# A four-layer decoder on one core: coefficient loads of the weight folding moved, half openings of the streamed attentions reordered, and the last experts' down product split into parts

## The reference

```
x = _layernorm(x + _L0_attn_ref(x, ...))      # minGRU, a gated scan
x = _layernorm(x + _L0_xattn_ref(x, ctx, ...))
x = _layernorm(x + _L0_ffn_ref(x, ...))       # butterfly: W_exp, 10 stages, gelu, 10 stages, W_con
x = _layernorm(x + _L1_attn_ref(x, ...))      # 16 heads of 16, causal
x = _layernorm(x + _L1_xattn_ref(x, ctx, ...))
x = _layernorm(x + _L1_ffn_ref(x, ...))       # 8 experts, top 2, gated, and a shared expert
x = _layernorm(x + _L2_attn_ref(x, ...))      # 16 heads of 16, no mask
x = _layernorm(x + _L2_xattn_ref(x, ctx, ...))
x = _layernorm(x + _L2_ffn_ref(x, ...))       # 8 experts, top 2, all computed
x = _layernorm(x + _L3_attn_ref(x, ...))      # window of 64
x = _layernorm(x + _L3_xattn_ref(x, ctx, ...))
x = _layernorm(x + _L3_ffn_ref(x, ...))       # 16 experts, top 4
```

```
def body(acc, expert):
    w1e, b1e, w2e, b2e, ce = expert
    hmid = jax.nn.gelu(x @ w1e + b1e, approximate=False)
    return (acc + (hmid @ w2e + b2e) * ce[:, None], None)
```

## Time and profile before

| what | us |
|---|---|
| median of three runs | 2581.3 |
| the three runs | 2581.3, 2587.81, 2570.56 |
| the profiled execution's own time | 2578.14 |
| its span | 2576.4 |
| PE busy in the span | 2279.8 |
| DVE busy in the span | 1404.3 |
| ACT busy in the span | 1129.9 |

### The profile page before, as it was taken

One profiled execution on the slowest core, in us unless ns is written; L12 is line 12 of the kernel. 1 busy time (PEld: TensorE's weight loads), 2 busy tenths in 40 slices (PEclk: granted clock), 3 DMA queues, 4 the chain that ended last, 5 costly groups with the idle time before them and its releaser, 6 DMA issues. The chain is left out here.

```text
span 2576.4 us, 41981 instructions
## 1 busy us (share of the span) xinstructions
PE 2279.8 (88%) x15258; PEld 1519.6 (59%) x15258; DVE 1404.3 (55%) x3517; ACT 1129.9 (44%) x1927; POOL 644.5 (25%) x868
## 2 busy tenths in 40 slices
PE   1789999998899999949999998799998898699996
PEld 1678754444345799924444444467665545589995
DVE  5625377885464221268999955666566555411114
ACT  6543345655342111135777774522443334234444
POOL 6010232321211033231111002100356311245551
PEclk8789978988998999967999999789999898799998
DMA  6100132220113199832131101031111210599996
GB/s 231 34 1 1 34 55 44 46 46 18 30 35 119 58 332 332 304 105 47 26 51 26 26 7 46 2 115 38 31 27 19 57 18 26 209 297 350 356 342 234
DMA packets 86512, 268.89 MB, mean 104 GB/s; under 512 B 25354, under 2 KB 43906, under 8 KB 70300
## 3 DMA queue, kind: packets, MB, share of 16 engines
q1 hardware_dynamic: 70628, 233.10, 29.6%
q0 software_dynamic: 15680, 33.12, 4.1%
HBM read 207.36 MB, written 23.94 MB: 90 GB/s over the span
## 5 line engine op out<-in xcount | busy, mean ns | idle before, releaser
L1667 ACT ACTIVATE prob<-st_ps 128x1024 f32<-128x1024 f32 x448 | 412.8, 933 | 215.3 <-PE st_ps L1534 213.9
L1687 DVE TENSOR_REDUCE cmax<-ring 128x1 f32<-128x512 f32 x640 | 401.4, 683 | 40.2 <-PE ring L1542 37.7
L3133 PE MATMUL A<-xbT,w 128*128 128x128 f32 x2512 | 301.8, 276 | 1.1 <-DMA w<-L1f_W_dram 0.5
L3133 PEld LDWEIGHTS A<-xbT,w 128*128 128x128 f32 x2512 | 291.6, 193 | 1.9 <-DMA w<-L1f_W_dram 0.8
L1581 PE MATMUL acc<-prob,v 128*32 128x256 f32 (+2 forms) x3200 | 265.5, 405 | 13.6 <-DVE byq L1725 12.6
L3377 DVE COPY yb<-C 128x256 f32<-128x256 f32 x118 | 50.1, 424 | 285.3 <-PE C L3141 282.4
L3050 POOL DMA_INDIRECT y_rows_dram<-yb,dst x118 | 116.3, 986 | 326.1 <-DVE yb L3377 322.9
L3141 PE MATMUL C<-w,hid 128*128 128x256 f32 x632 | 149.3, 379 | 0.0
L1534 PE MATMUL st_ps<-qst,kst 64*128 64x512 f32 (+3 forms) x560 | 135.6, 482 | 7.3 <-DMA qst<-parts 3.2
L3037 POOL DMA_INDIRECT xb<-x_rows_dram,src x118 | 115.0, 975 | 99.7 <-DVE src L3347 64.4
L1683 DVE CUSTOM_DVE_ANT_0 masked<-ring,causal_wide 128x512 bf16<-128x512 f32 (+3 forms) x256 | 112.5, 487 | 44.2 <-PE ring L1542 43.3
(11 more groups left out here) (478 smaller groups left out, 4471.0 us busy)
## 6 DMA issues: line engine op xcount, KB each, us to landing
w<-L3f_W_dram SPq DMA_DIRECT2D x79, 1026.0 KB
w<-L1f_W_dram SPq DMA_DIRECT2D x39, 1536.0 KB
room<-y_rows_dram SPq DMA_DIRECT2D x8, 1024.0 KB, 10.1
kst<-parts SPq DMA_DIRECT2D x120, 64.0 KB, 2.4
qst<-parts SPq DMA_DIRECT2D x120, 64.0 KB, 2.4
gate<-L2f_gates_dram SPq DMA_DIRECT2D x5, 1536.0 KB, 7.4
first<-parts SPq DMA_DIRECT2D x96, 64.0 KB, 2.4
qT<-dense SPq DMA_DIRECT2D x84, 64.0 KB, 2.4
```

The lines of the kernel that those rows point to most:

```text
L1667: act.activation(prob[:, step % PROBS, 2 * p:2 * p + 2, 0:n], st_ps[:, p, :, 0:n], ACT.Exp, scale=scale)\
L1687: dve.tensor_reduce(cmax[:, a, t:t + 1, k0 // CH], spot(key)[:, 0:k1 - k0], AX.X, ALU.max)\
L3133: mm = pe.matmul(A[:, j % 2 * 2 + a, f * TB:(f + 1) * TB], up_w(w[:, j % WB], a, k, f), xbT[:, j % 2, k, :], start=(k == 0), stop=(k == KT ...
```

## The change

There are three parts.

**Folding.** The ring of `coef_d` grows from 2 to 6. The order of SP's loads is written anew: coefficients come earlier and `x` and `ctxT` come last.

```
-    coef_d = sbuf(nc, st, "coef_d", [P, 2, 2, NB8, SUB])
+    RU, RD = 3, 6
+    coef_d = sbuf(nc, st, "coef_d", [P, RD, 2, NB8, SUB])
...
         down_coefs(1, 1)
-        up_coefs(1, 2)
+        up_coefs(1, 1)
+        down_coefs(2, 2)
+        up_coefs(2, 1)
+        down_coefs(4, 1)
         sp.dma_start(down_rows[:, :, :], dram["W_con"]).then_inc(s.down_loaded, 16)
+        up_coefs(3, 1)
         begin.load_x(sp, 2)
         begin.load_x(sp, 3)
-        for i in range(3):
-            down_coefs(2 + i, 1)
-            up_coefs(3 + i, 1)
+        up_coefs(4, 1)
...
-        begin.load_pads(sp)
-        down_coefs(STEPS, 2)
+        up_coefs(5, 1)
+        down_coefs(5, 5)
+        up_coefs(6, 2)
```

```
                 for step in range(NS):
                     c = step + LEAD if step + LEAD < NC else None
-                    group(step, 0, c)
+                    opening = step > LAG and opens[(step - LAG) % nS]
+                    scores(step, 0)
+                    if c is not None:
+                        pieces(c, 1)
+                    if opening:
+                        scores(step, 1)
                     if step >= LAG:
                         weigh(step - LAG, False)
-                    group(step, 1, c)
+                    if not opening:
+                        scores(step, 1)
+                    if c is not None:
+                        pieces(c, 0)
...
+                    for n in turns_due(c):
+                        key = ("turn", n)
+                        act.wait_ge(s.act_filled, filled(key))
+                        if n >= 2:
+                            act.wait_ge(c_loaded[n % 2], 32 * (n // 2))
+                        act.activation(crow[:, n % 2, :], spot(key)[0:HU * TH, 0:P], ACT.Copy).then_inc(s.act_freed, 1)
...
                     if c is not None:
-                        pieces(c, (0, 1))
+                        pieces(c, (0,))
                     if closing(step - LAG):
                         turned(step - LAG)
+                    if c is not None:
+                        pieces(c, (1,))
```

```
+            def drop_in_parts(j):
+                pe.wait_ge(s.down_low, j + 1)
+                pe.wait_ge(s.hid_low, j + 1)
+                to = room_c(("drop", j))
+                for f in range(NF):
+                    cols = slice(f * D, (f + 1) * D)
+                    pe.matmul(to, hid_hi[:, j % 2, f, :], down_hi[:, j % 2, cols], start=(f == 0), stop=False)
+                    pe.matmul(to, hid_hi[:, j % 2, f, :], down_lo[:, j % 2, cols], start=False, stop=False)
+                    mm = pe.matmul(to, hid_lo[:, j % 2, f, :], down_hi[:, j % 2, cols], start=False, stop=(f == NF - 1))
+                mm.then_inc(s.down_done, 1)
...
+            def raise_down(j):
+                act_e.wait_ge(w_ready[j % WB], 16 * (j // WB + 1))
+                if j >= 2:
+                    act_e.wait_ge(s.down_done, j - 1)
+                act_e.activation(down_hi[:, j % 2, :], down_rows(j), ACT.Copy).then_inc(s.down_high, 1)
...
                     if j >= 2:
-                        act_e.wait_ge(s.down_done, j - 1)
+                        act_e.wait_ge(s.hid_low, j - 1)
...
                     a.then_inc(s.hid_ready, 1)
+                    if j + 1 < NBLK:
+                        raise_down(j + 1)
...
+            def lower_down(j):
+                dve.wait_ge(s.down_high, j + 1)
+                dve.tensor_tensor(down_lo[:, j % 2, :], down_rows(j), down_hi[:, j % 2, :].bitcast(F32), ALU.subtract).then_inc(s.down_low, 1)
+
+            def part_hid(j):
+                dve.wait_ge(s.hid_ready, j + 1)
+                if j >= 2:
+                    dve.wait_ge(s.down_done, j - 1)
+                dve.tensor_copy(hid_hi[:, j % 2], hid[:, j % 2]).then_inc(s.hid_high, 1)
+                dve.wait_ge(s.hid_high, j + 1)
+                dve.tensor_tensor(hid_lo[:, j % 2], hid[:, j % 2], hid_hi[:, j % 2].bitcast(F32), ALU.subtract).then_inc(s.hid_low, 1)
...
             for j in range(NBLK):
+                if biased:
+                    part_hid(j)
+                    if j + 1 < NBLK:
+                        lower_down(j + 1)
```

More of the change, by code:

```diff
@@ L614, in chain @@
             stride = 2 ** (STEPS - 1 - t if down else t)
-            now = coef_d[:, i % 2] if down else coef_u[:, i % 3]
+            now = coef_d[:, i % RD] if down else coef_u[:, i % RU]
             own, par = now[:, 0], now[:, 1]
@@ L1535, in group, with pieces @@
                                        start=True, stop=True, skip_group_check=True)
-                        if side:
-                            mm.then_inc(s.s_ready, 1)
-                    for side in range(2 if chunk else 0):
-                        key = ("piece", c, 2 * (1 - p) + side)
+                    mm.then_inc(s.s_ready, 1)
+                def pieces(c, pair):
+                    gm = c // nC
+                    if pair == 1 and c in (0, TH):
+                        front.await_copies(pe, c // TH)
+                    elif pair == 1 and c % nC == 0:
+                        pe.wait_ge(*stacks_done(gm))
+                    t, k0, k1, _ = chunks[c % nC][0]
+                    for side in range(2):
+                        key = ("piece", c, 2 * pair + side)
                         room(key)
                         rows = slice(64 * side, 64 * side + HP)
-                        pe.matmul(spot(key)[:, 0:k1 - k0], stack_of(0, gm)[rows, 1 - p, t * P:(t + 1) * P],
-                                  stack_of(1, gm)[rows, 1 - p, k0:k1], start=True, stop=True, skip_group_check=True).then_inc(s.dve_filled, 1)
+                        pe.matmul(spot(key)[:, 0:k1 - k0], stack_of(0, gm)[rows, pair, t * P:(t + 1) * P],
+                                  stack_of(1, gm)[rows, pair, k0:k1], start=True, stop=True, skip_group_check=True).then_inc(s.dve_filled, 1)
                 def extras(c):
@@ L1590, in _ @@
                 for c in range(LEAD):
-                    for p in range(2):
-                        group(None, p, c)
+                    pieces(c, 1)
+                    pieces(c, 0)
                     extras(c)
@@ L2928, in routed_moe @@
         else:
[L2929 to L2930 removed]
+            act, hid = None, flat_xT[:, (XB + 4) * D:(XB + 4) * D + 2 * NF * TB].rearrange("p (x f n) -> p x f n", x=2, f=NF)
+            hid_hi = sbuf(nc, st, "hid_hi", [P, 2, NF, TB], F32R)
+            hid_lo = sbuf(nc, st, "hid_lo", [P, 2, NF, TB], F32R)
+            down_hi = sbuf(nc, st, "down_hi", [P, 2, NF * D], F32R)
+            down_lo = sbuf(nc, st, "down_lo", [P, 2, NF * D], F32R)
+        yb = flat_xT[:, XB * D:(XB + 4) * D].rearrange("p (x d) -> p x d", x=4) if biased else sbuf(nc, st, "yb", [P, 4, D])
         room = sbuf(nc, st, "room", [P, RU * PAIR * K * D])
```

95 lines of the change are left out of this document (45 added, 50 removed).

## The result

The changed kernel takes 2555.86 us (median of 6 runs, 2554.42 to 2568.37), the kernel before 2579.41 (median of 6, 2570.56 to 2587.81). The ratio is 0.9909, with a 95% interval of 0.9886 to 0.9932: 23.5 us or 0.9% faster. It lies inside the forecast range, on the forecast side, and 6 us above the forecast value. It is just short of the 1% from which the forecast counted a change as told apart, but the interval excludes no change.

The account below looks back on a forecast made before the run. PE and DVE were taken to bound the unmasked attention, PE with DMA close behind the last experts, table waits the start. -16 - 1.5 - 6.5 - 7.5 = -31.5 on 2578.1 gives 2546.6, by the median 2550; range 2541 to 2559.

Parts of the forecast that it names:

- I count on both fitting in: Start: the masks and the first product's trip through DRAM fit into 7 us of room; the start gains 16.
- 28.2 less 2 to the end: Start: up_lo ends 28.2 us behind the start of con_hi, and L684 moving up gives some 2 more.
- the start gives only its first wait: Rival, start: another thing holds the second product, so the start gives 6 us, whole 2560; chance 0.10.
- half of a cast's and a stall's sum: Unmasked attention: half of 4.3 us of casts plus 10.7 of stall, 7.5, less 1 for ACT, gives -6.5.
- -4, nothing but the casts: Unmasked attention: bound of the gain at 4 us if only the casts count; the other bound was -11.
- Steady blocks: Last experts: 3.50 us per block for 3.73, over 58 blocks, -13 us.
- 0.117 per matmul: Last experts: half the 0.234 us of a 512-column fp32r matmul, so the drop's 12 matmuls take 1.40.
- The bound of 2.58: Last experts: the drop's upper bound if 256-column matmuls can't beat 0.215 us; the skill's weight-load rule pointed toward it.
- the chain is longer: ... 4.3 to 4.4: Last experts, 16 blocks with a settle: the chain takes 4.3 to 4.4 us for 4.51; effect 0, from -2 to +8.
- Tail: Last four expert blocks: ACT, with diagonals and high parts at 5.0 us per block, becomes the bound, about +4.
- near 3.4: Last experts: DMA busy 3.58 us per block is no hard floor, but a floor near 3.4 is likely.
- The rival of POOL shut out: Last experts: POOL can't run beside DVE's 2.33 us, its period is 4.57, whole 2611; 0.08 together with slow drop.

Follow-up runs that it names:

- e_hold: Changed kernel with DVE's low part of w2 put behind the copy to yb and the settle; last experts 369.7 us against 380.1.
- e_moe: Kernel before with the new last experts alone; 2575.45 us in one run against 2576.17, last experts 375.8 against 388.9.
- e_tail: Changed kernel with the last-blocks edit: fp32 drop of before, without the parts' work, in the last three blocks; last experts 377.1 us against 380.1.
- the combined kernel: Changed kernel with masks early, low part of w2 behind the copy, fp32 drop in last three blocks; 2534.87 us, ratio 0.9828 to the kernel before.
- e_pads: Changed kernel with the padding mask loads right behind the last five down-side tables, ahead of two up-side tables; start 100.4 us against 105.4.
- e_order_old: Changed kernel with PE's old order at the attention openings, second pair's scores behind the value product; unmasked attention 408.9 us against 409.7.
- e_turned_old: Changed kernel with DVE's transpose of the sums back behind both pieces; unmasked attention 410.3 us against 409.7.
- e_crow_dve: Changed kernel with the copy of the turned maxima back on DVE; unmasked attention 410.9 us against 409.7.
- e_half: Changed kernel with only the first half of w2's low part computed from block 2 on; last experts 373.8 us against 380.1.

## Why the prediction was right or wrong

The mechanism and the sign were right in all three parts. The sum was 8 us too large by the medians. In the two profiles it was 9.1: 5.0 at the start, 3.6 in the unmasked attention and 2.0 in stages that the change doesn't touch, less 1.3 that the experts gave beyond the forecast and 0.3 of the causal one. That the total still came within 6 us is in part luck: the changed kernel's profile has the better of two starts, and the late blocks in its experts vary by some us from run to run.

**The start, -16 forecast, -11.0 measured.** The failed step is "I count on both fitting in". The room of 7 us for the masks and the trip through DRAM was worked out rightly: DVE's third table had to start by 57.44 - 14.2 = 43.2. But the masks' loads stand behind a table of the up side that waits for a buffer, were issued only from 35.98 on, and DVE got on at 43.35 with two more tables to go. Its third table began at 47.06, 3.8 late, and `con_hi` was 4.2 late. I named the mask loads and gave them 2 us as the lower bound without asking which wait stood ahead of them in SP's queue. With them moved, 55.8 and 81.9 came out as forecast, so the rest of the working (the first chain 5.2 shorter, ACT's own list next, 28.2 less 2 to the end) holds. In the changed kernel the first spread began at 20.5, 4.6 earlier than before where 5.2 was forecast. The next block took 72.8 us, 72.7 before, so `x` and `ctxT` behind everything else cost nothing that shows. The rival "the start gives only its first wait" was the right place, with half its size.

**The unmasked attention, -6.5 forecast, -2.9 measured.** The failed step is "half of a cast's and a stall's sum". The stall of 10.7 us did go, and the 4.3 us of casts left DVE. DVE's waits for PE rose from 17.5 to 20.4 us. The second bound, "-4, nothing but the casts", was the nearer one. In this stage, with both engines busy to 96%, taking away a wait of 10.7 and 4.3 of work was worth 2.9. The runs that undo single pieces moved the stage by 1.2 us or less in either direction, so what each piece is worth stays open within the scatter.

**The causal attention, -1.5 forecast.** The profile shows -1.8. One execution can't bear that out, since the same code took 331.3 to 340.8.

**The last experts, -7.5 forecast, -8.8 measured.** Term by term:

- Steady blocks: 3.50 forecast, 3.44 measured. PE's own 3.41 nearly holds. The price of 0.117 per matmul from half of a 512-column one was right (0.12), so the drop came to 1.4 to 1.5. The bound of 2.58 and with it the rule on weight loads (the Trainium skill, TensorE: Matmul & The Clock Gate, "What overlaps and what doesn't") isn't borne out. All rows are full in each of these matmuls, and they start 0.12 apart though each has its own load.
- Blocks with a settle: 0 forecast, +0.05 each measured. The chain was named rightly in its last links, but I took it as covered. `e_hold` shows that it was the bound, with 0.36 per block to be had. The step that failed here is "the chain is longer: ... 4.3 to 4.4", which came out at 4.56.
- Tail: +4 forecast. From the fourth-last lift to the end of the last drop it is 22.3 us where it was 17.0, so 5.3. In `e_moe` and `e_hold` it is 20.0, so 3.0 is the price of the parts. The last-blocks edit takes 2.9 of it back, as the combined kernel against `e_hold` shows. The other 2.3 are the late load of weights (1.1) and the last drop (1.2). It ran at half the pace, after a wait of PE for `hid_lo`:

```profile
2509.67 0.55 PE L3163 MATMUL C<-down_hi,hid_hi 128*128 128x256 f32 x1 [2.64 <-DVE hid_lo L3433]
2510.02 0.42 PE L3164 MATMUL C<-down_lo,hid_hi 128*128 128x256 f32 x1
2510.24 0.41 PE L3165 MATMUL C<-down_hi,hid_lo 128*128 128x256 f32 x1
```

  Its matmuls start 0.21 apart instead of 0.12. The granted clock is 0.50 there, the lower of PE's two (1.2 of 2.4 GHz):

```profile
2509.60:2512.60 3.00, 2.90 (x12) 2.64 (x12) 0.31 (x1) 2.40 (x5) 0.97 (x1) 0.50 0.13 46
```

  In `e_hold` PE was idle for 2.63 us at the same place and kept its clock and the 0.12.
- Not forecast: single late blocks of 3.7 to 4.8 us, about 3 us in all in the changed kernel, 5 in `e_pads`, 0.8 in `e_moe` (one of 4.22). With the tail's 2.3 this makes the difference between `e_moe` (-13.1) and the changed kernel (-8.8). Part of them are loads that landed late while the DMA engines were 0.95 busy, which fits the forecast's floor "near 3.4". In `e_pads` six blocks waited for their weights, all behind 2430 us, and five of them in a row were 4.1 to 5.1 apart:

```profile
PE A L3153 <- DMA w<-L3f_W_dram: 3.8, 6, 1.5
```

  In the changed kernel the block of 4.38 waited 0.73 for gathered rows from DRAM, and the first of the tail 0.96 for weights. The DMA engines' busy time per block fell from 3.58 to 0.95 x 3.44 = 3.27 for the same loads, so it is no hard floor, as the forecast said.

**The rival of POOL shut out** was right about the delay and wrong about its weight. The gather waits for DVE's instruction (1.73 for 0.97, 0.83 left after DVE's end). The Trainium skill (SBUF — State Buffer, "Who interferes with whom") says that a DVE instruction with two SBUF inputs contends with a GpSimd instruction that reads SBUF. This agrees. The same place says that in its own measurement a `tensor_tensor` didn't stall a DMA, and here it delays an indirect one by 0.76 us. But only one of POOL's two instructions per block is hit in the changed kernel: the scatter has a median of 1.00. In `e_hold`, where `down_lo` stands behind the copy, it is the other one (gather 0.97, scatter 1.72 by the medians). With 1.73 + 1.1 + 0.6 for gaps POOL comes to 3.43 per block, which is just PE's pace, and 0.2 more than the forecast's 3.2. In the rival it was 4.57. The forecast also counted 2.33 of DVE's work as two-input. The 0.43 of it that writes `hid_hi` has one input, which leaves 1.90.

**What stays open.** In the long block at 2429 us of the changed kernel ACT stood idle 2.73 us in front of a gelu whose input was there after some 0.4:

```profile
2429.62 1.14 ACT L3271 ACTIVATE xT<-A,w 128x128 f32<-128x128 f32 x4 [2.73 <-DMA first<-parts]
```

The releaser named there is a load of an earlier stage and can't be it. `e_tail`, `e_hold`, `e_order_old`, `e_turned_old` and the combined kernel have ACT idle for 1.8 to 3.8 us at nearly the same instruction of ACT's program, `e_moe` doesn't. One guess is that ACT's own instructions arrive late while the DMA engines are 0.95 busy. The runs speak against a fixed place in ACT's program. `e_moe` and `e_crow_dve` both have an ACT program that is shorter by the 32 copies of the maxima, and `e_crow_dve` shows the wait all the same, at the same block:

```profile
2442.80 1.14 ACT L3271 ACTIVATE xT<-A,w 128x128 f32<-128x128 f32 x4 [3.07 <-DMA first<-parts]
```

So the cause stays open. The long blocks of `e_pads` are another matter, waits for weights as told above, and those of `e_half` are mostly short ones of 3.5 to 3.7 that no run explains.

## What to carry to other kernels

When a load is moved back in a queue, ask what wait stands ahead of its new place, and find its first user on every engine. Four small mask loads cost 5 to 7 us here because tables that wait for a buffer lay in front of them. When new work is given to an idle engine, put it behind whatever frees a buffer for the next step: DVE was idle most of the time, and 1.2 us in the wrong place still set 16 blocks. In a stage where two engines are both at 96%, don't count on half of what is removed from either: here 15 us of waits and work gave 2.9. And before a median is read as the effect of an edit, look for it in a kernel without the edit: the gathers of 0.97 in `e_half` were in `e_pads` too.

## What the runs showed of the hardware that was not expected

- An indirect DMA issue on POOL that begins while a two-input DVE instruction runs ends 0.82 to 0.88 us after that instruction (334 of 334 in eleven kernels, counted as said above), and it does so block after block: 1.73 us for 0.97. One that began first was hardly touched, at most 1.23 us, even when DVE followed 0.1 us behind. The phase matters more than the share: DVE was at such work for 1.9 of the 3.4 us of a block, and in `e_pads` neither of the two issues was delayed in most blocks.
- Twelve fp32r matmuls of 256 columns take 1.4 to 1.5 us where the same product in fp32, four matmuls in eight records, took 1.72. Three products in fp32r are thus no more than a fifth cheaper than one in fp32.
- An unchanged stage, the causal attention, took from 331 to 341 us in single profiled executions, with a granted clock of 0.81 and 0.84 in its first half in the two that were compared.
